# A four-layer graph network kernel on one Trainium2 core: weights loaded first, a rebuilt start of the edge sort, and a scatter whose last ten spans need no copies

## The reference, cut to what matters

```
L0: neigh = segment_sum(h[src], dst) / max(deg, 1); layernorm(h @ W_self.T + neigh @ W_neigh.T + b)
L1: two GCN convolutions, out[v] = b + sum dinv[u] * w * dinv[v] * (x W)[u], then a row norm
L2: m = relu([h[src], edge_attr] @ W1.T + b1) @ W2.T + b2; agg = segment_sum(m, dst); GRU(agg, h)
L3: agg = segment_sum(h[src] * w1, dst); agg @ W.T + b
each layer gets h, the normalised and rectified x, and its result is added to x
```

## Time and profile before

| | us |
|---|---|
| median of 3 runs | 1371.41 (1367.62 to 1372.83) |
| the profiled execution's own time | 1371.79 |
| its span, first to last instruction | 1370.0 |

### The profile page before, as it was taken

One profiled execution on the slowest core, in us unless ns is written; L12 is line 12 of the kernel. 1 busy time (PEld: TensorE's weight loads), 2 busy tenths in 40 slices (PEclk: granted clock), 3 DMA queues, 4 the chain that ended last, 5 costly groups with the idle time before them and its releaser, 6 DMA issues.

```text
span 1370.0 us, 20255 instructions
## 1 busy us (share of the span) xinstructions
PE 1192.8 (87%) x4298; PEld 745.9 (54%) x4298; DVE 1016.8 (74%) x2113; ACT 572.2 (42%) x1461; POOL 700.4 (51%) x828
## 2 busy tenths in 40 slices
PE   5468499429999999999998899999999899998998
PEld 2343244214444445558876555454454588886787
DVE  9796845129999998642387688898888899888433
ACT  0221121027777730220011388787788833334211
POOL 0577777768888843776676366666666100000000
PEclk9679699859999999999999999999999999999999
DMA  8851512130000036333226677776777200002231
GB/s 331 313 197 40 199 63 79 55 113 18 27 20 25 12 146 223 112 114 131 82 88 181 204 224 221 223 234 207 226 213 221 58 1 0 1 0 89 77 96 37
DMA packets 87258, 167.89 MB, mean 123 GB/s; under 512 B 16124, under 2 KB 44670, under 8 KB 84644
## 3 DMA queue, kind: packets, MB, share of 16 engines
q1 hardware_dynamic: 59588, 102.69, 22.5%
q0 software_dynamic: 25472, 59.97, 14.4%
q10 hardware_dynamic: 2144, 4.59, 1.0%
HBM read 115.96 MB, written 51.23 MB: 122 GB/s over the span
## 4 chain that ended last, share of the span: by engine, by line
PE 62%; POOL 14%; issue 10%; DVE 8%; DVEq 2%; DMA 2%; ACT 1%; POOLq 0%; SPq 0%; ACTq 0%
PE pb L1348 11%; POOL cell_rows L720 10%; PE pb L1248 6%; PE pb L1240 6%; PE pb L1443 5%; PE pb L1213 5%; PE pb L1416 4%; PE pb L1418 4%; PE pb L1417 4%; PE pb L1362 3%; PE pb L1364 2%; PE pb L1365 2%; PE pb L1123 2%; PE pb L1341 2%; DMA p_rows<-tiles 2%
## 5 line engine op out<-in xcount | busy, mean ns | idle before, releaser
L765 POOL DMA_INDIRECT dst_rows<-ering,gidx x168 | 171.7, 1022 | 101.3 <-issue 95.4
L1348 PE MATMUL pb<-arena 128*128 128x512 f32 x368 | 191.2, 602 | 14.1 <-ACT arena L990 13.8
L720 POOL DMA_INDIRECT cell_rows<-tiles,gidx x168 | 166.8, 993 | 68.1 <-issue 47.4
L819 POOL DMA_INDIRECT arena<-p_rows,arena x96 | 100.5, 1047 | 78.6 <-issue 24.9
L1213 PE MATMUL pb<-arena 128*128 128x384 f32 x268 | 96.7, 504 | 42.4 <-POOL arena L772 42.2
L875 ACT ACTIVATE arena<-iota,free 128x128 f32<-128x128 f32 x266 | 92.3, 394 | 85.9 <-DMA free<-cell_rows 39.2
L1917 DVE TENSOR_TENSOR arena<-pb,arena 128x512 f32<-128x512 f32 x184 | 122.3, 683 | 5.7 <-DMA arena<-p_rows,arena 3.3
L1924 DVE SCALAR_TENSOR_TENSOR low<-arena,high 128x512 fp32r<-128x512 f32 x138 | 95.2, 690 | 31.4 <-ACT high L997 22.0
L819 POOL DMA_INDIRECT arena<-p_rows,ws x88 | 89.1, 1013 | 53.9 <-issue 29.0
L1213 PE MATMUL pb<-tiles,arena 128*128 128x384 f32 x264 | 94.4, 501 | 15.2 <-DVE arena L1761 9.4
L1759 DVE TENSOR_TENSOR arena<-pb,arena 128x192 f32 x266 | 94.1, 354 | 12.8 <-PE pb L1213 12.7
(11 more groups left out here) (331 smaller groups left out, 2550.6 us busy)
## 6 DMA issues: line engine op xcount, KB each, us to landing
dst_rows<-arena SPq DMA_DIRECT2D x6, 2046.0 KB, 17.5
ering<-in_edge_attr_dram SPq DMA_DIRECT2D x41, 256.0 KB
arena<-adj SPq DMA_DIRECT2D x10, 640.0 KB, 4.1
arena<-dst_rows SPq DMA_DIRECT2D x24, 264.0 KB
arena<-wt_gru SPq DMA_DIRECT2D x48, 128.0 KB
ws<-dst_rows SPq DMA_DIRECT2D x22, 264.0 KB
arena<-in_x_dram SPq DMA_DIRECT2D x18, 256.0 KB, 7.8
arena<-in_L_gnn_W_hh_dram SPq DMA_DIRECT2D x3, 1024.0 KB
```

Of the source, the lines that this page charges most:

```text
L720: nc.gpsimd.indirect_dma_start(cell_rows[:, :], bass.IndirectOffsetOnAxis(gidx[:, SPAN * a + k:SPAN * a + k + 1], 0), cring[:, a, k], None ...
L765: nc.gpsimd.indirect_dma_start(dst_rows[:, :], bass.IndirectOffsetOnAxis(gidx[:, k:k + 1], 0), ering[:, k, :], None).then_inc(e_scattered[ ...
L819: nc.gpsimd.indirect_dma_start(rows[:, k % GROUP, :], None, p_rows[:, :], bass.IndirectOffsetOnAxis(edge_rows(k).bitcast(I32)[:, 0, DE:DE ...
L1348: nc.tensor.matmul(e_bank(k)[:], erowT[:, k % 4], w1e_sb, start=True, stop=True).then_inc(edge_mm, 1)
```

## The change

- **Order of SP's work.** The weight loads come right after the edge loads. The zeros for `cell_rows` (2 DMAs) follow the second weight load, those for `dst_rows` (now 24 DMAs of about half a megabyte) the tenth; all take zeros from `ering` (1056 elements) and no longer from `h` (5120). The stores of the products m and c, and then the loads of x, come after that.
- **One-hots.** One `tensor_scalar` for each of the 168 columns, 102 bf16 elements against one value per partition (`cell_f`), in place of the four broadcasts. B1 is 102.
- **Counts.** One matmul per span (`before`); `total` comes from one matmul with `last_row` afterwards. PE turns the first weight block ahead of all counts.
- **Bases.** Four instructions fewer in the chain. `row_of` is made by ACT, `own` by POOL and ACT (`apart`), `sum_spans(0)` and the payload's integers are moved off the chain.
- **Batches.** The first two batches are one span each. In all there are seven instead of five.
- **Weights.** The three blocks that are multiplied get places of their own (`ih_turned`), and the products come after all ten blocks.
- **Scatter.** Spans 0 to 23 go as before. The last ten read `idx1` and `pay1` in place, in straight-line code; the empty column 167 is left out.

The diff, cut to its core:

```diff
-        B1 = CELLS + 1
+        B1 = CELLS + 2
-        O_PARTS = [0, 9, 18, 27, SPANS]
-        BATCHES = [0, 2, 6, 14, 24, SPANS]
-        SUMMED = [0, 2, 6, 10, 14, 19, 24, 29, SPANS]
+        O_PARTS = [0, 9, 18, 26, 31, SPANS]
+        BATCHES = [0, 1, 2, 4, 8, 14, 24, SPANS]
+        SUMMED = [0, 1, 2, 4, 8, 11, 14, 19, 24, 29, SPANS]
...
+            for k in range(DST_ZEROS):
+                sp.dma_start(dz[:, k * dst_zeros:(k + 1) * dst_zeros], zeros[:, 0:dst_zeros]).then_inc(zeroed, 16)
...
+            pool.wait_ge(cells_known, 1)
+            for d in range(1, SPAN):
+                nc.gpsimd.tensor_tensor(apart[:, d - 1, :, d:], cell5[:, :, d:], cell5[:, :, 0:SPAN - d],
+                                        ALU.subtract).then_inc(own_apart, 1)
+            pool.wait_ge(own_equal, 2)
...
+            pool.wait_ge(order_ready[0], len(BATCHES) - 1)
+            passed()
+            for span in range(BATCHES[-2], SPANS):
+                pool.wait_ge(c_scattered[span % 2], 16 * SPAN * (span // 2))
+                passed()
+                for j in range(SPAN * span, min(SPAN * span + SPAN, USED)):
+                    nc.gpsimd.indirect_dma_start(cell_rows[:, :], bass.IndirectOffsetOnAxis(idx1[:, j:j + 1], 0),
+                                                 pay1[:, j], None).then_inc(c_scattered[span % 2], 16)
...
+            act.wait_ge(row_known, 1)
+            nc.scalar.activation(row_of, iob_f[:, 0:SPANS].unsqueeze(2).to_broadcast([P, SPANS, P]), ACT.Abs,
+                                 bias=row_p).then_inc(row_ready, 1)
+            act.wait_ge(own_apart, SPAN - 1)
+            apart_flat = apart.rearrange("p d g j -> p (d g j)")
+            nc.scalar.activation(apart_flat, apart_flat, ACT.Abs).then_inc(own_equal, 1)
+            act.wait_ge(own_equal, 1)
+            nc.scalar.activation(apart_flat, apart_flat, ACT.Relu, bias=1.0, scale=-1.0).then_inc(own_equal, 1)
+            act.wait_ge(row_ready, 1)
+            nc.scalar.activation(row_of, row_of, ACT.Relu, bias=1.0, scale=-1.0).then_inc(row_ready, 1)
...
+            pe.wait_ge(const_ready, 9)
+            turn_weights(0)
             pe.wait_ge(sort_const, 1)
...
+            pe.wait_ge(counts_summed, 1)
+            nc.tensor.matmul(dve_bank("total")[:, 0:B1], last_row, before, start=True, stop=True).then_inc(for_dve, 1)
+            pe.wait_ge(base_ready, 2)
+            pe.wait_ge(row_ready, 2)
+            rank_spans(0)
+            turn_weights(1)
+            rank_spans(1)
+            rank_spans(2)
+            rank_spans(3)
+            turn_weights(2)
...
-                vtt(oh1[:, c], iob[:, 0:B1].unsqueeze(1).to_broadcast([P, n, B1]),
-                    cell_b[:, c].unsqueeze(2).to_broadcast([P, n, B1]), ALU.is_equal).then_inc(hot1_ready, 1)
+                for j in range(SPAN * O_PARTS[q], min(SPAN * O_PARTS[q + 1], J)):
+                    ins = vts(oh1[:, j], iob[:, 0:B1], cell_f[:, j:j + 1], None, ALU.is_equal)
+                ins.then_inc(hot1_ready, 1)
...
+            nc.vector.tensor_reduce(before, whole(dve_bank("before")), AX_X, ALU.add).then_inc(dve_read, 1)
+            dve.wait_ge(dve_read, V["before"] + 1)
+            dve.sem_inc(counts_summed, 1)
...
+            vts(cnti, dve_bank("total")[:, 0:B1], float(P - 1), None, ALU.add).then_inc(dve_read, 1)
```

More of the change, by code:

```diff
@@ L46 @@
 COL = 8
[L47 removed]
+USED = JV + 1
+J = -(-USED // COL) * COL
 PAIR = 2 * P
@@ L415, in build_gnn @@
         act_jobs = []
-        for n, (name, third) in enumerate(blocks):
+        for n in range(len(blocks)):
             act_jobs += [("w", n, k) for k in range(5 if n == 0 else KT)]
-            if blocks[n - 1][0][0:2] == "ih":
-                act_jobs += [("m", blocks[n - 1][1], k) for k in range(KT)] + [("c", blocks[n - 1][1])]
+        for gate in range(3):
+            act_jobs += [("m", gate, k) for k in range(KT)] + [("c", gate)]
         for t in range(NT + 1):
@@ L491, in _ @@
             column(w1t_t, w1_in.rearrange("e a -> (e a)"), edges_loaded)
[L493 to L502, removed]
-            for n, (name, third) in enumerate(blocks):
-                if n == X_AFTER:
-                    sp.wait_ge(sorted_all, 1)
-                    sp.wait_ge(x_free, 1)
-                    for t in range(NT):
-                        m = P if t + 1 < NT else LAST
-                        sp.dma_start(xs[0:m, t], x_in[t * P:t * P + m, :]).then_inc(xe_loaded[t], 16)
+            for n, (name, third) in enumerate(blocks):
                 if n >= 2:
@@ L1144, in count_span @@
                 n = columns(g) * B1
-                for job, left in (("before", later[:, SPANS - 1 - g:SPANS - 1 - g + P]), ("total", ones_b)):
-                    ins = nc.tensor.matmul(dve_bank(job)[:, 0:n], left, hot_span(g, columns(g)), start=g == 0, stop=g == SPANS - 1)
-                    if g == SPANS - 1:
-                        ins.then_inc(for_dve, 1)
+                ins = nc.tensor.matmul(dve_bank("before")[:, 0:n], later[:, SPANS - 1 - g:SPANS - 1 - g + P],
+                                       hot_span(g, columns(g)), start=g == 0, stop=g == SPANS - 1)
+                if g == SPANS - 1:
+                    ins.then_inc(for_dve, 1)
             def rank_spans(n):
@@ new lines, in _, with fold @@
+            turn_weights(5)
+            rank_spans(6)
+            turn_weights(6)
+            turn_weights(7)
+            rank_spans(7)
+            turn_weights(8)
+            rank_spans(8)
+            turn_weights(9)
+            def fold(gate, products):
+                for k in products:
+                    job = ("m", gate, k) if k < KT else ("c", gate)
+                    b = to_act(job)
+                    for o in range(KT):
+                        left = w2_raw[:, o, k * P:(k + 1) * P] if k < KT else b2_wide[:, o]
+                        ins = nc.tensor.matmul(b[:], left, ih_turned[:, gate, o], start=o == 0, stop=o == KT - 1)
+                    ins.then_inc(for_act, 1)
```

244 lines of the change are left out of this document (124 added, 120 removed).

## The result

| | before | after |
|---|---|---|
| median, us | 1372.12 (1367.62 to 1373.95, 4 runs) | 1412.81 (1411.24 to 1416.5, 4 runs) |
| profiled span, us | 1370.0 | 1411.2 |
| mean granted clock | 0.953 | 0.933 |

The ratio is 1.0299, with a 95% interval of 1.0271 to 1.0326: slower by some 41 us, where 1363 us and a gain of 8.9 had been forecast. It is outside the range and on the side that had been given 0.07.

A forecast was written before the change was run, and what follows sets the result against it. Bound: POOL issuing 168 indirect DMAs, set by the first scatter's start and the row's length. First scatter 1.3 us earlier plus row 7.6 us shorter is 8.9: 1371.8 - 8.9 = 1362.9, so 1363 us; eight-in-ten range 1352 to 1372.

The forecast's parts named there:

- one-hots begin: DVE's start of the sort: first one-hot at 5.8 us instead of 8.4, 2.6 us less, bounds 0 and 2.6.
- one-hots: DVE's 168 comparisons at 0.155 us: 26.0 us, 8.0 more than before, plus 0.5 for sharing with POOL.
- last one-hot to reduce: End of the one-hots to the counts' reduce, with one PE matmul a span: 1.3 us, 2.9 less.
- reduce to first scatter: Chain of bases, ranks and places up to POOL's first scatter: 9.0 us, 4.3 less, bounds 3.3 and 5.
- row of scatters: POOL's 168 indirect DMAs: ten shorter gaps, 6.3 us, and the empty column, 1.3; together 7.6 us less.
- The sum: First scatter 1.3 us earlier plus 7.6 us from the row: 8.9 us less, 1363 us.
- Everything moved beside this I cost at nothing: Work moved outside the sort chain and the scatter row, such as the products and x, was priced at 0 us.
- the cover of the stage with x: This stage ended 28 us before the sorted edges and would lose at most 8.9 us of that lead.
- The gain hidden behind the stage with x: Rival: the stage with x ends last, so no gain shows, about 1371 us; chance 0.03.
- the shut-out: Rival: DVE's dense one-hots block POOL's subtractions, first scatter 15.7 us later than before, 1380 us; chance 0.06.
- the zeros: Rival: 12.6 MB of zeros slow the scatters beside them, 16 us lost at half pace, 1379 us; chance 0.05.
- the two rivals on the stream: One-hot pitch: 0.10 us, 1354 us, chance 0.25; or 0.185 to 0.23, 1368 to 1376 us, chance 0.13.

The follow-up runs named there:

- experiment 1: Changed kernel with its last ten spans back in the loop with copies, still without the empty column: 1392.75 us, ratio 1.0161.
- Experiments 7: Kernel before, last ten spans straight and in place, a small memset and a wait for it ahead of each: 1368.86 us, ratio 0.9964.
- 14: Kernel before, last ten spans straight and in place, a pause after every 25 scatters: 1373.46 us, ratio 1.002.
- 4: Kernel before with one edit, its last ten spans in a straight line and in place, without pauses: 1382.47 us, ratio 1.0071.
- 8: Kernel before, last ten spans straight and in place, each waiting for the landing of the span just before it: 1380.29 us, ratio 1.0073.
- 2: Changed kernel, last ten spans still in a straight line but with rows and indices copied first: 1393.79 us, ratio 1.0169.
- experiments 3: Changed kernel with the 168 one-hot comparisons put back into five broadcast ones: 1390.72 us, ratio 1.0146.
- 5: Changed kernel with its last ten spans in loops and 93 one-element DVE memsets ahead of the block loop: 1368.43 us, ratio 0.9982.
- 9: Kernel before with 48 one-element DVE memsets ahead of the block loop: 1378.57 us, ratio 1.0176.
- 10: Changed kernel with a memset and wait between the spans in place, and 93 DVE memsets ahead of the block loop: 1350.2 us, ratio 0.9963.
- 12: Changed kernel, all 34 spans straight and in place, a pause ahead of each, 93 DVE memsets ahead of the block loop: 1346.99 us, ratio 0.9932.
- experiments 9 to 12: The third chip's runs: 9, 10, 12, and the kernel before with its last ten spans in place and a pause every ten scatters, 1350.28 us.

## Why the prediction was wrong

By its own steps, forecast and then measured:

| step | forecast | measured |
|---|---|---|
| one-hots begin | 5.8 | 6.04 |
| one-hots | 26.0 + 0.5 us | 27.6 us |
| last one-hot to reduce | 1.3 | 1.2 (33.66 to 34.90) |
| reduce to first scatter | 9.0 | 9.05 |
| first scatter | 42.6 | 43.95 |
| row of scatters | 7.6 us shorter | 10.4 us shorter (236.7 for 247.1) |
| end of the row | 8.9 us earlier | 10.3 us earlier |

**The sum was right and was not the time.** Its largest miss is the row, 2.8 us: the gap turned out at the lower bound of 0.30 (8.2 us for the 6.3 taken), and spans 0 to 23 took 0.7 us less, though they had been left as they were. Two misses offset one another in the end of the row, a first scatter 1.35 us later than forecast and the shorter row. The step that failed is "Everything moved beside this I cost at nothing", at two places that it did not look at.

**The row was costed on POOL alone.** Its ten gaps were priced at what they cost POOL (6.3 us), and the cover of the stage with x was held against a loss of 8.9 us of cover. That cover was real: in experiment 1, with the later loads, DVE is through at 268.73 and the load of the sorted edges is issued at 289.88. What was not asked is what the gaps did for others. Without them PE's increments came up to 48.8 us late, the stage stood still for most of 60 us, and the line "If this stage came 20 us later, it would be what is late next" describes what happened: it came 50 us later, and the blocks 18.0 us. Experiments 7 and 14 show it by the pause alone, 4 and 8 beside them; 2 shows that the loop is not needed for a quick stage, and 7 that the copies are not.

**The one-hots were costed by their time and not by their length.** The duration was forecast within 1.1 us. That 168 instructions in the place of four move all later code of DVE, and that a loop some 600 instructions further on would be fetched anew in every turn, was in no term and in no rival: 24 us (experiments 3, 5 and 9). That the move decides is shown; that the code is fetched anew is read from the count of instruction packets and the holes.

**The rivals.** The gain hidden behind the stage with x was named and given 0.03, with a time of 1371; it was right in the place, wrong in the size, and without the cause. The slower outcome had 0.07 in all, for other reasons (the shut-out, the zeros), so that chance foretold nothing of this. The shut-out of POOL did not happen in the changed kernel and did in experiment 3. The zeros did nothing to the row (its turns in the loops kept their gap). The pitch of 0.164 us put an end to the two rivals on the stream. "VectorE: DVE Perf Modes" of the Trainium skill, TRN2 errata, would have had 0.087 us an instruction; measured is 0.164, so its figure is too low for this instruction. Whether the pointer makes the difference, as the prediction took it, or the mode, no run shows.

**What stays of the change.** With both causes away it gives 0.2% in loops (experiment 5, an interval that just takes in no change), 0.4% with the pause (10), and 0.7% with the whole row in place (12, which goes beyond the change); the sum had 0.65%. The last two are from the third chip. Experiment 7, the kernel before with its last ten spans in place and a pause, has 0.4% too: the rebuilt start of the sort, whose first scatter came no earlier (43.95 for 43.85), adds nothing that these runs can tell.

**Open.** Why a dense row of indirect DMAs makes PE's increments late, and why one of three chips shows none of it, was not found. Shown is that it is no lack of instruction packets in that stretch, no DMA load, and no matter of loop, copies or place of the payload. It is not settled how many may follow each other: five with a pause of 0.9 us did no harm over the last ten spans on the second chip, 25 with the same pause left the stage with x standing still there, as 47 to 48 without one did elsewhere, and ten held up everything over the whole row. Ten over the last spans, and five over the whole row, were tried only on the chip without late increments. That the place of the loop counts modulo 128 instructions is a guess from packets of 8192 bytes that foretold experiments 5 and 9; positions 12, 34 and 127 were quick, 47 slow, in the programs that were tried, and the width of the slow part is not known.

## What to carry to other kernels

A gap on an engine that sets the end may be what the others live on: before a row of POOL's indirect DMAs is packed, keep a short pause after every few (five and 0.9 us here), and look at the other engines' waits for PE and for "remote", not at the row alone. Measure such a change on more than one chip: on one of the three here no increment was late in any run. When instructions are added or taken away ahead of a long loop on the same engine, compare the count of instruction packets in the profile; if it jumps and a hole returns once in every turn, shift the loop with a few idle instructions before believing anything else about the change. And broadcast comparisons of several microseconds on DVE can cost a POOL helper ten times its own duration (experiment 3); the 168 short ones with one tensor did not.

## What the runs showed of the hardware

- Beside a row of indirect DMAs at a pitch of 1.27 us, with 0.30 us between them, PE's semaphore increments arrived 1.4 to 48.8 us after the end of their instruction, later and later along the row (changed kernel), while those of DVE, ACT and POOL arrived within 0.01 us. With a gap of 0.9 us after every five none found was over 0.7 us late (experiment 7), with an idle wait of 1.9 us none over 0.6 (8).
- The third chip had no late increments of PE (none over 0.3 us up to 1300 us in experiments 9 to 12) and ran the kernel before in 1355.4 us, against 1370.8 to 1372.7 on the two others.
- A DVE loop of 32 chunks in a turn of 28 us ran its turn without or with a hole of 3.7 to 4.0 us, depending on how many instructions stood ahead of it: 639, 652, 802, 908 without, 687 and 815 with. The hole comes with 30 more instruction packets and costs 24 us over the 266 chunks.
- Three POOL subtractions of 34 to 102 elements took 4.4 to 5.1 us each beside DVE comparisons with two tensor inputs of 4.5 to 5.1 us (all four 14.76 us), and all four 1.21 us beside comparisons of 0.164 us with one tensor and a pointer.
